# Four stages of an audio tower on one core: rows loaded at the head of the queue's turn, a scale in a register, loops written out, attention with deeper buffers

## The reference, cut to what matters

```python
def _L0_ffn_ref(x, ...):            # on _layernorm(h)
    up = silu(einsum('td,edh->teh', xt, Wu) + bu)
    gt = einsum('td,edh->teh', xt, Wg) + bg
    act = up * gt * w_full[:, :, None]
    y = einsum('teh,ehd->td', act, Wd) + w_full @ bd      # and a shared expert, the 17th
...
def _L1_attn_ref(x, ...):           # on _layernorm(h); 12 heads of 16, 525 rows
    q, k, v = ...
    attn = einsum('bhnd,bhmd->bhnm', fake_quant(q), fake_quant(k)) * scale
    attn = softmax(attn, axis=-1)
    out = einsum('bhnm,bhmd->bhnd', fake_quant(attn), fake_quant(v))
    ... fake_quant(out) @ fake_quant(w_proj) + b_proj
```

## Time and profile before

| | us |
|---|---|
| median of 3 runs | 5021.34 (5014.97 to 5021.38) |
| the profiled execution | 5018.49, its span 5016.8 |
| PE busy | 3730.5 (74%) |
| DVE busy | 3504.8 (70%) |
| ACT busy | 2718.9 (54%) |
| POOL busy | 1604.2 (32%) |
| mean granted clock of TensorE | 0.787 |

### The profile page before, as it was taken

One profiled execution on the slowest core, in us unless ns is written; L12 is line 12 of the kernel. 1 busy time (PEld: TensorE's weight loads), 2 busy tenths in 40 slices (PEclk: granted clock), 3 DMA queues, 4 the chain that ended last, 5 costly groups with the idle time before them and its releaser, 6 DMA issues. The chain is left out here.

```text
span 5016.8 us, 79151 instructions
## 1 busy us (share of the span) xinstructions
PE 3730.5 (74%) x23684; PEld 2834.3 (56%) x23732; DVE 3504.8 (70%) x7340; ACT 2718.9 (54%) x5075; POOL 1604.2 (32%) x1365
## 2 busy tenths in 40 slices
PE   0069999994999999999528677777677743489990
PEld 0059999993898888889514311111122223489990
DVE  7749888894666666666577599999677755645552
ACT  4535555552444444444335699999788833434430
POOL 4647777772333333334200000000000022422216
PEclk9999999996999999999755655555555555589995
DMA  3235455443222222222233700000111156233325
GB/s 99 78 104 144 130 151 140 139 138 101 75 75 75 75 75 75 75 75 73 82 100 90 248 22 21 21 21 15 62 64 64 64 170 216 89 102 114 105 88 155
DMA packets 294150, 478.09 MB, mean 95 GB/s; under 512 B 62419, under 2 KB 224187, under 8 KB 281938
## 3 DMA queue, kind: packets, MB, share of 16 engines
q1 hardware_dynamic: 274066, 448.83, 29.1%
q0 software_dynamic: 16896, 19.40, 1.4%
q10 hardware_dynamic: 2944, 6.99, 0.6%
HBM read 354.24 MB, written 123.73 MB: 95 GB/s over the span
## 5 line engine op out<-in xcount | busy, mean ns | idle before, releaser
L693 PE MATMUL b_pA<-b_woutT,b_ys 128*105 128x192 f32 x3840 | 689.6, 327 | 1.2 <-ACT b_ho L579 0.4
L976 POOL TENSOR_TENSOR c_ap<-c_ac,c_ap 128x420 fp32r<-128x420 f32 x340 | 428.2, 1259 | 772.5 <-ACT c_ap L1121 772.0
L1909 ACT ACTIVATE g_pS<-g_pS,g_stt,k_cs 128x525 f32<-128x525 f32 x816 | 627.4, 837 | 8.1 <-DVE g_junk L1936 7.5
L1936 DVE TENSOR_SCALAR_CACHE_REDUCE g_junk<-g_pS,g_csn 128x525 bf16<-128x525 f32 x816 | 606.7, 764 | 32.8 <-PE g_pS L1891 24.5
L693 PEld LDWEIGHTS b_pA<-b_woutT,b_ys 128*105 128x105 f32 x3840 | 610.8, 171 | 12.2 <-ACT b_ho L579 3.9
L1891 PE MATMUL g_pS<-g_qk 16*128 16x262 bf16 (+1 forms) x1536 | 462.2, 408 | 157.3 <-ACT g_pS L1909 141.3
L491 POOL TENSOR_TENSOR b_ys<-b_hs,b_cb 128x525 f32<-128x525 f32 x384 | 507.0, 1321 | 222.3 <-DVE b_hs L776 179.4
L1121 ACT ACTIVATE c_ap<-c_ac 128x420 fp32r<-128x420 f32 x340 | 189.2, 556 | 661.0 <-DVE c_ac L1253 659.3
L776 DVE TENSOR_TENSOR_SCAN b_hs<-b_ae,b_pB 128x525 f32<-128x525 f32 x384 | 479.1, 1248 | 39.8 <-ACT b_ae L606 5.1
L1041 PE MATMUL c_pD<-cw_wd,c_ap 128*105 128x192 f32 x4080 | 440.7, 257 | 18.5 <-POOL c_ap L976 18.5
L1041 PEld LDWEIGHTS c_pD<-cw_wd,c_ap 128*105 128x105 f32 x4080 | 426.9, 173 | 42.5 <-POOL c_ap L976 30.3
(11 more groups left out here) (384 smaller groups left out, 7977.5 us busy)
## 6 DMA issues: line engine op xcount, KB each, us to landing
b_cb<-dram_ct SPq DMA_DIRECT2D x64, 1050.0 KB, 8.3
c_wb<-dram_wt SPq DMA_DIRECT2D x60, 840.0 KB, 10.7
b_cb<-dram_ct SPq DMA_DIRECT2D x64, 525.0 KB, 7.0
c_wb<-dram_wt SPq DMA_DIRECT2D x20, 1050.0 KB
dram_qk<-f_qk SPq DMA_DIRECT2D x16, 787.5 KB, 6.0
g_qk<-dram_qk SPq DMA_DIRECT2D x16, 787.5 KB, 4.6
h_qk<-dram_qk SPq DMA_DIRECT2D x16, 787.5 KB
dram_o<-h_oT SPq DMA_DIRECT2D x16, 787.5 KB, 3.5
```

The lines of the kernel that those rows point to most:

```text
L693: ins = pe.matmul(into, ys[:, u % RING, t * TP:(t + 1) * TP], woutT[:, u % NU, :], start=(u == 0 and t % 2 == 0), stop=(u % NU == NU - 1), ...
L976: nc.gpsimd.tensor_tensor(ap[LO][:, r, :], ac[:, r, :], ap[HI][:, r, :].bitcast(F32), ALU.subtract)\
L1909: nc.scalar.activation(x, x, ACT.Exp, bias=stt[:, k, 0, c:c + 1], scale=K["cs"][:, 0:1], accum_out=stt[:, k, 1, c:c + 1]).then_inc(s["exp" ...
L1936: v.tensor_scalar(junk[:, (q + k) % 2, :], pS[:, q % RING, OFF:OFF + S], csn[:, 0:1], 3.0e38, ALU.mult, ALU.min, accum_out=stt[:, k, 0, c: ...
```

## The change

In the experts' stage SyncE calls `rows(c + 3)` first in its turn. In the statistics pass the scale of the exponential is read once into a register of ScalarE; VectorE takes the plain negated maximum of a tile into `raw`, and GpSimd multiplies it by the scale into `stt`, where ScalarE reads its bias; all loops are written out. In the attention pass the scale is in a register too, the exponentials have three buffers (`EXR`) and the probabilities four (`PRR`), TensorE combines three steps behind (`BEHIND`) in place of two, VectorE's evacuations come one step later, the maxima of the output thirds go to 48 columns of `om` that are merged once at the end, and the loops are written out. In both passes ScalarE's table is loaded ahead.

```diff
             def body(c, i, k, last):
+                rows(c + 3)
                 sp.wait_ge(s_out[k], i * 16)
                 sp.dma_start(y[:, k, :, :], tiles(h1, c)).then_inc(s_y[k], 16)
                 if last < 2:
                     weights(c + 1, range(len(GROUPS)))
-                rows(c + 3)
                 store(c, k)
...
# statistics pass, GpSimd
+                for q in range(NQ):
+                    c = column(q)
+                    pool.wait_ge(s["max"], at(b, NQ, q + 1))
+                    if q == 0:
+                        pool.wait_ge(s_o[k], i * 144)
+                    pool.tensor_tensor(stt[:, k, 0, c:c + 1], raw[:, k, c:c + 1], K["cs"][:, 0:1],
+                                       ALU.mult).then_inc(s["mn"], 1)
# statistics pass, ScalarE
+            cs = act.alloc_register("g_cs")
+            act.reg_load(cs, K["cs"][0:1, 0:1].bitcast(I32))
+            act.preload_act_table(ACT.Exp)
...
-                    nc.scalar.activation(x, x, ACT.Exp, bias=stt[:, k, 0, c:c + 1], scale=K["cs"][:, 0:1],
+                    nc.scalar.activation(x, x, ACT.Exp, bias=stt[:, k, 0, c:c + 1], scale=cs,
                                          accum_out=stt[:, k, 1, c:c + 1]).then_inc(s["exp"], 1)
# statistics pass, VectorE
-                dve.wait_ge(s_o[k], i * 144)
+                dve.wait_ge(s["mn"], at(b, NQ, -NQ))
...
-                    dve.wait_ge(s["mn"], at(b, NQ, q - 1))
-                    v.tensor_scalar(junk[:, (q + k) % 2, :], pS[:, q % RING, OFF:OFF + S], csn[:, 0:1], 3.0e38, ALU.mult,
-                                    ALU.min, accum_out=stt[:, k, 0, c:c + 1]).then_inc(s["mn"], 1)
+                    v.tensor_reduce(raw[:, k, c:c + 1], pS[:, q % RING, OFF:OFF + S], AX, ALU.max, negate=True)\
+                        .then_inc(s["max"], 1)
# both passes, all engines
-            two_a_turn(act, NB, body)
+            written_out(NB, body)
# attention pass
-        ex = sb("ex", [128, 2, 3 * QM])
-        pr = sb("pr", [128, 2, 3 * QM], BF16)
+        BEHIND, EXR, PRR = 3, 3, 4
+        ex = sb("ex", [128, EXR, 3 * QM])
+        pr = sb("pr", [128, PRR, 3 * QM], BF16)
...
-            for k in range(2):
-                body(k, 0, k, k == 0, 0)
-            with eng.Fori(1, NB // 2 - 1) as i:
-                ...
+            for b in range(NB):
+                body(b, b // 2, b % 2, b == 0, max(0, b - (NB - 3)))
# TensorE
-                    if n >= 2:
-                        combine(b, i, k, n - 2)
+                    if n >= BEHIND:
+                        combine(b, i, k, n - BEHIND)
# ScalarE
+            act.preload_act_table_set("natural_log_exp_and_others")
...
-                    act.wait_ge(s["P"], at(b, TN, n - 1))
+                    act.wait_ge(s["P"], at(b, TN, n + 1 - EXR))
# VectorE
                 dve.wait_ge(s["Rv"], at(b, HG, g + 1))
+                if g == 0:
+                    dve.wait_ge(s_o[k], b // 2 * 16)
...
-                v.tensor_reduce(om[:, :], oT[:, k, g, :], AX, ALU.max, apply_absolute_value=True).then_inc(s_om, 1)
-                dve.wait_ge(s_om, b * HG + (g + 1))
-                v.tensor_tensor(K["amax"][:, 7:8], K["amax"][:, 7:8], om[:, :], ALU.max).then_inc(s["om"], 1)
-                dve.wait_ge(s["om"], at(b, HG, g + 1))
+                c = b * HG + g
+                v.tensor_reduce(om[:, c:c + 1], oT[:, k, g, :], AX, ALU.max, apply_absolute_value=True)\
+                    .then_inc(s["om"], 1)
...
-                    if n == 1 and not first:
+                    if n == BEHIND - 1 and not first:
                         evacuate(b - 1, i + k - 1, 1 - k, 2)
-                    if n in (7, 13):
-                        evacuate(b, i, k, 0 if n == 7 else 1)
+                    if n in (5 + BEHIND, 11 + BEHIND):
+                        evacuate(b, i, k, 0 if n == 5 + BEHIND else 1)
                     dve.wait_ge(s["E"], at(b, TN, n + 1))
-                    wait_combined(dve, b, n - 2)
+                    if n >= PRR or not first:
+                        wait_combined(dve, b, n - PRR)
...
-            dve.sem_inc(s_m0, 1)
+            dve.wait_ge(s["om"], at(NB - 1, HG, HG))
+            v.tensor_reduce(K["amax"][:, 7:8], om[:, :], AX, ALU.max).then_inc(s_m0, 1)
```

More of the change, by code:

```diff
@@ L1816, in attention_heads @@
         pS = ctx.enter_context(nc.psum_tensor("g_pS", [128, RING, 1024], F32))
-        s_m0, s_all, s_v, s_go, s_i, s_c, s_k, s_qt = (sem(n) for n in (
-            "s_m0", "s_all", "s_v", "s_go", "s_i", "s_c", "s_k", "s_qt"))
+        s_m0, s_all, s_v, s_go, s_i, s_k, s_qt = (sem(n) for n in (
+            "s_m0", "s_all", "s_v", "s_go", "s_i", "s_k", "s_qt"))
         s_q = [sem(f"s_q{k}") for k in range(2)]
         s_o = [sem(f"s_o{k}") for k in range(2)]
-        s = {n: sem("q_" + n) for n in ("S", "mn", "exp", "min")}
+        s = {n: sem("q_" + n) for n in ("S", "max", "mn", "exp", "min")}
         block = ctx.enter_context(nc.Block())
@@ L1849, in _ @@
                 load(k, 0, k)
-            two_a_turn(sp, NB, turn)
+            written_out(NB, turn)
             for k in range(2):
@@ L1908, in body @@
                     x = pS[:, q % RING, OFF:OFF + S]
-                    nc.scalar.activation(x, x, ACT.Exp, bias=stt[:, k, 0, c:c + 1], scale=K["cs"][:, 0:1],
+                    nc.scalar.activation(x, x, ACT.Exp, bias=stt[:, k, 0, c:c + 1], scale=cs,
                                          accum_out=stt[:, k, 1, c:c + 1]).then_inc(s["exp"], 1)
-            two_a_turn(act, NB, body)
+            written_out(NB, body)
         @block.vector
         def _(dve):
-            for n in ("mn", "min"):
+            for n in ("max", "min"):
                 dve.sem_inc(s[n], CREDIT)
             dve.wait_ge(s_i, 4)
-            v.tensor_scalar(csn[:, :], K["cs"][:, 0:1], -1.0, None, ALU.mult).then_inc(s_c, 1)
-            dve.wait_ge(s_c, 1)
             def lowest(b, k):
@@ L1972, in attention_heads @@
         pR = ctx.enter_context(nc.psum_tensor("h_pR", [128, QM], F32))
-        s_m0, s_all, s_v, s_go, s_i, s_k, s_om, s_st, s_ln, s_a = (sem(n) for n in (
-            "s_m0", "s_all", "s_v", "s_go", "s_i", "s_k", "s_om", "s_st", "s_ln", "s_a"))
+        s_m0, s_all, s_v, s_go, s_i, s_k, s_st, s_ln, s_a = (sem(n) for n in (
+            "s_m0", "s_all", "s_v", "s_go", "s_i", "s_k", "s_st", "s_ln", "s_a"))
         s_in = [sem(f"s_in{k}") for k in range(2)]
@@ L2154, in _ @@
             batches(pe, body)
-            for n in range(TN - 2, TN):
+            for n in range(TN - BEHIND, TN):
                 combine(NB - 1, NB // 2 - 1, 1, n)
@@ L2167, in body @@
                     act.wait_ge(s["S"], at(b, TN, n + 1))
-                    act.wait_ge(s["P"], at(b, TN, n - 1))
-                    nc.scalar.activation(ex[:, (n + k) % 2, :], pS[:, (n + k) % 2, :, :].rearrange("p t l -> p (t l)"),
-                                         ACT.Exp, scale=K["cs"][:, 0:1]).then_inc(s["E"], 1)
+                    act.wait_ge(s["P"], at(b, TN, n + 1 - EXR))
+                    nc.scalar.activation(ex[:, (b * TN + n) % EXR, :], pS[:, (n + k) % 2, :, :].rearrange("p t l -> p (t l)"),
+                                         ACT.Exp, scale=cs).then_inc(s["E"], 1)
                     if n - 1 in REST:
@@ L2174, in body @@
                         act.wait_ge(s["Pr"], at(b, HG, g))
-                        nc.scalar.activation(exr[:, :], pR[:, 0:W], ACT.Exp, scale=K["cs"][:, 0:1]).then_inc(s["Er"], 1)
-            two_a_turn(act, NB, body)
+                        nc.scalar.activation(exr[:, :], pR[:, 0:W], ACT.Exp, scale=cs).then_inc(s["Er"], 1)
+            written_out(NB, body)
         @block.vector
```

26 lines of the change are left out of this document (12 added, 14 removed).

## The result

| | before | after |
|---|---|---|
| median of 4 runs each | 5021.36 us | 4854.6 us (4851.9 to 4856.03) |
| the profiled execution, its span | 5018.49, 5016.8 | 4856.03, 4854.3 |
| PE, DVE, ACT, POOL busy | 3730.5, 3504.8, 2718.9, 1604.2 | 3741.1, 3431.6, 2597.6, 1768.4 |
| mean granted clock | 0.787 | 0.794 |

The ratio is 0.967 (0.9654 to 0.9687): 167 us less, where 154 were forecast (4867). TensorE's busy time is the same within 11 us, VectorE's and ScalarE's are 73 and 121 us less, GpSimd's is 164 more; where the time went is seen stage by stage only. First the windows of the changed stages, to be held against the earlier trace rows: 17 chunk periods of the experts, the statistics pass from its first exponential to its last, the attention pass likewise. Columns: length; then busy time of PE, weight loads, DVE, ACT, POOL; the granted clock; DMA share; GB/s.

A forecast was written before the change was run, and what follows sets the result against it. Each stage was read alone: TensorE 94% busy in the experts, ScalarE the statistics pass's bound, no engine full in attention. Gains of 38 + 71 + 45 = 154 us from 5018.5 gave 4864.5, adjusted to 4867; range 4822 to 4938.

The forecast's parts named there:

- 17 periods of 59.4: Experts: loading rows first shortens each chunk period from 61.66 to 59.4 us, 38 us in all, bounds 31 and 40.
- the chunk without a statistics load: Experts: the period after the 17 with VectorE's wait, 59.28 us, taken as the basis for the new period.
- The column's price: Statistics pass: reading scale from a [128,1] column costs ScalarE 0.09 us a step, bounds 0 and 0.10.
- Who sets the step: Statistics pass: ScalarE still sets the time per tile, 0.680 us in place of 0.767.
- the ring: Statistics pass: a tile's round through four PSUM slots and the engines, 2.60 us with GpSimd's hop, 0.65 a step.
- VectorE's new step: Statistics pass: VectorE's plain maximum in place of multiply-and-minimum, 0.65 us a tile, under ScalarE's.
- The two batch terms: Statistics pass: added per batch, 0.5 us for VectorE's `lowest` at tile 7 and 0.6 for the first three tiles.
- rival D: Statistics pass: GpSimd's hop makes the kernel slower; at 1.5 us a hop the whole takes 5087 us; chance 0.04.
- the 5 us for the maxima: Attention pass: estimated gain from 48 multiplications of VectorE's maxima that go with their waits, 0.1 us each.
- TensorE's sum: Attention pass: TensorE's busy time, evacuation wait, issue and 0.8 us of exponential waits make a batch of 28.7 us.
- Rival B: Attention pass gains only its low end, 25 us, because TensorE's order at half clock holds it: 4887 us; chance 0.15.
- Rival C: Attention pass: denser TensorE is granted full clock, ScalarE's 24.6 us a batch binds, gain 106: 4806 us; chance 0.07.

The follow-up runs named there:

- rows_only: Kernel before with only the load rows(c + 3) moved first in SyncE's turn; 4978.4 us, ratio 0.9924.
- hop2: Kernel after with two more 128 x 1 multiplies on GpSimd ahead of each one that ScalarE waits for; 4873.1 us, ratio 0.9711.
- hook_warm: Kernel of hook with one more unused 128 x 1 GpSimd multiply in the stage before the statistics pass; 4826.5 us, ratio 0.9599.
- attn_shallow: Kernel after with two exponential buffers, two probability buffers and combining two steps behind in the attention pass; 4881.4 us, ratio 0.9731.
- written_only: Kernel before with only the loops of the statistics and attention passes written out, no table loaded ahead; 4996.0 us, ratio 0.9953.
- hook: Kernel after with TensorE doing rest products or the next fill before waiting for the evacuation, in three of 17 attention steps; 4826.9 us, ratio 0.9617.
- attn_b2e3p3: Kernel after with combining two steps behind and three probability buffers in the attention pass, three exponential buffers kept; 4852.4 us, ratio 0.9665.

## Why the prediction was right

**Experts.** Forecast 17 periods of 59.4 and 38 us; measured 59.22, which is 41.4 us over the 17, more than the bound of 40. Between the stage's first and last matmul only 38.2 are left, since the first chunk was 3.0 longer at its lower clock: that this meets the 38 is luck. rows_only, without that loss, gained 40.9 in the stage (39.3 in the medians). Reading the period from the chunk without a statistics load was the right way, and adding 0.12 for the work that it lacked was too careful: that work fitted beside matmuls entirely.

**The column's price.** Forecast 0.09 from two groups of another stage; measured 0.092.

**Who sets the step.** Forecast 0.680 (0.677 and a little), ScalarE's; measured 0.674, ScalarE's. The parts under it: multiply 0.2 us forecast, 0.191 measured; multiply to exponential 0.3 forecast, 0.31 measured; the ring 2.60 forecast, 2.51 by hop2. VectorE's new step was put at 0.65; with GpSimd out of the way its first tiles in hook_warm came 0.61 to 0.62 apart. The two batch terms (0.5 for `lowest`, 0.6 for the first tiles) have the right sum and the wrong parts: in each batch one exponential start is 0.2 late at tile 7 and one 0.9 at the batch's change, 1.1 together. So the pass was forecast at 573 and took 568 between the same two points; from the first matmul it gained 70.2, and the forecast said 71.

**Where two errors met.** The start cost 5 us that I had at nothing: I had written that GpSimd's block product falls beside VectorE's first maximum, without asking why it stood 10.8 us late in the trace of before (a wait for TensorE by the view, but 7.4 us behind a MODIFY_POOL_CONFIG too). There it was hidden, since nothing but the rest tiles waited for it; the change put GpSimd on the path of every tile. The step, 0.006 shorter than forecast, paid it back: 816 x 0.006 = 5.

**Which edit earned it.** Here the forecast leaned on a wrong picture. It took the register, the maximum and the hop as one thing, with VectorE's old instruction at 0.71 as a reason for the new one. Alone, the register gives 57.5, the loops 8.5; for the maximum with its hop and the table loaded ahead 4 are left by difference (no run has register and loops with VectorE's old instruction), and the parts agree: 816 x (0.685 - 0.674) = 9, less the 5 of the start. The risk that I named rival D was taken for 4 us of gain.

**Attention.** Forecast 28.7 a batch, 28.4 with the 5 us for the maxima, and 45 us in all; measured 454.91/16 = 28.43, and 45.9 from the first matmul to the last. By the runs: depth 24.8 (attn_shallow), loops 9.5 (written_only), and by difference 11.6 for the register, the merged maxima and the table loaded ahead. TensorE's sum, 24.6 busy + 2.4 evacuation + 0.9 issue + 0.8, was the right one to make, and hook shows its second term as a price. But its first term lacked the 48 products that the trace of before hasn't, and the 0.9 "issue" was their place and no wait: after has 25.7 busy, 2.1 evacuation, 0.5 for the exponentials and no such issue. The two misreadings cancel, since 24.6 + 0.9 = 25.5. The forecast that combining a step later helps is refuted (attn_b2e3p3): only the buffers do. Rival B was right in that TensorE's order holds the batch, but it holds it at 28.4 and not at the low end, 25 us of gain. Rival C: the clock stayed at 0.50 even with TensorE busy 96% (hook); its premise of 79% before was 83%.

**The rest.** The forecast's 154 us are 154.3 in the three stages of the profiled execution. In that sum the experts' 38.2 hold the 3.0 lost at the lower clock of the first chunk, so the changed code earned some 157. The 8 us more came in the router's stage (4.4), the projection's (1.4) and the last layer of experts (2.0), and the median is 12.4 under the forecast. Nothing in the forecast allowed for stages whose code is the same.

## What to carry to other kernels

An operand of one column on ScalarE is worth 0.09 us an instruction: where it is the same for all partitions and ScalarE sets the step, a register alone gives it back, and the other engines' own speed is then to be measured, since their gapless rows may show only its pace. Of depth, add one buffer of each kind and measure; of a wait for a single bank that the leading engine pays in full, fill it with that engine's own later work. Before putting GpSimd on a path, look for how late its first instruction of the kind comes, and let it do one in an earlier stage. Count the matmuls of a stage against another trace before taking TensorE's busy time or an "issue" wait at its word. A stage that comes out as forecast is to be split once more: here all three did so by errors that cancelled in part.

## What the runs showed of the hardware

- The lower clock at 96% busy: the attention pass of hook has TensorE busy 413.15 of 429.01 us at a granted 0.50 (1.2 GHz), while the experts, 96% busy in the kernel after (969.58 of 1006.83), have 1.00 (2.4 GHz). The Trainium skill (TensorE: Matmul & The Clock Gate, Part 1) has sustained activity release the gate; the experts agree and this stage, just as busy by the rows, does not. Why stays open.
- GpSimd: 128 x 1 multiplies take 0.19 us each and go 0.14 us apart in a row; from MODIFY_POOL_CONFIG to the first multiply after a reduction over the partitions it was 8.4 (hook_warm; 6.8 to 9.3 in all traces), to the reduction after multiplies 5.9 (after; 5.6 to 6.0 in the nine traces in which the reduction waits for nothing else).
- The first chunk of the experts, the same work everywhere, took 64.4 to 64.6 us at a granted 0.94 in ten traces, 67.5 and 67.6 at 0.89 in two, 68.8 and 68.9 at 0.88 in two.
- The router's stage, the same code everywhere, took 174.8 to 185.4 us in the fourteen traces at the same clock of 0.50; what sets it stays open.
